# A graph network on one Trainium2 core: an attention table built head by head in other PSUM banks, and routing with bf16 counts and one-hots shared by two engines

## What is computed

```python
# layer 0 attention, 4 heads
f1 = einsum('hno,ho->hn', support, weight_u)      # support = inputs @ weight, by heads
f2 = einsum('hno,ho->hn', support, weight_v)
w = leaky_relu(f1[:, None, :] + f2[:, :, None], 0.2)
e = where(adj != 0, exp(w * adj - row_max), 0)
out = (e / sum(e)) @ support + ...
# layer 0 experts: 16, the best 2 for each row
gate_logits = x @ gate_w + gate_b
topk_vals, topk_idx = top_k(gate_logits, 2)
topk_w = softmax(topk_vals)
y = x + sum_k topk_w * (relu(x @ w1[e_k] + b1[e_k]) @ w2[e_k] + b2[e_k])   # then a layer norm
```

## Time and profile before

| | us |
|---|---|
| median of 3 runs | 2665.99 |
| lowest, highest | 2665.8, 2669.86 |
| the profiled execution | 2668.27 |
| its span, first to last instruction | 2666.3 |
| mean granted TensorE clock in the span | 0.964 |

### The profile page before, as it was taken

One profiled execution on the slowest core, in us unless ns is written; L12 is line 12 of the kernel. 1 busy time (PEld: TensorE's weight loads), 2 busy tenths in 40 slices (PEclk: granted clock), 3 DMA queues, 4 the chain that ended last, 5 costly groups with the idle time before them and its releaser, 6 DMA issues. The chain is left out here.

```text
span 2666.3 us, 57932 instructions
## 1 busy us (share of the span) xinstructions
PE 2475.0 (93%) x20164; PEld 2013.1 (76%) x20165; DVE 1996.3 (75%) x4252; ACT 1622.0 (61%) x3061; POOL 1422.0 (53%) x1705
## 2 busy tenths in 40 slices
PE   7799999999976997189999999999799999999999
PEld 6477777777755997176777777777588888888887
DVE  6799999999935443888877777777677777777775
ACT  1677777777731332246666666666577777777775
POOL 8566666666342553522222221112278888888886
PEclk9899999999987999599999999999799999999999
DMA  3011111111063223301111111110000000000001
GB/s 101 22 43 64 43 43 43 64 44 43 22 227 138 71 70 93 103 7 43 43 42 42 42 45 59 42 42 21 7 0 0 0 0 0 0 0 0 0 0 42
DMA packets 43751, 114.01 MB, mean 43 GB/s; under 512 B 5509, under 2 KB 29806, under 8 KB 37870
## 3 DMA queue, kind: packets, MB, share of 16 engines
q1 hardware_dynamic: 38062, 97.16, 10.4%
q0 software_dynamic: 5568, 15.21, 1.9%
HBM read 99.20 MB, written 13.15 MB: 42 GB/s over the span
## 5 line engine op out<-in xcount | busy, mean ns | idle before, releaser
L2270 PE MATMUL f_pm<-f_wl,f_yt 128*128 128x256 f32 x2640 | 625.4, 380 | 1.9 <-DVE f_gg L2099 1.9
L2270 PEld LDWEIGHTS f_pm<-f_wl,f_yt 128*128 128x128 f32 x2640 | 477.0, 191 | 54.0 <-issue 2.4
L1144 POOL TENSOR_TENSOR ADJ<-ADJ,OFF 128x2708 f32<-128x2708 f32 x21 | 125.3, 5965 | 539.7 <-DVE ADJ L1224 539.7
L120 POOL TENSOR_SCALAR f_yy<-f_th,f_rs 128x255 f32<-128x255 f32 x660 | 370.7, 577 | 21.8 <-POOL f_rs L115 21.8
L2099 DVE SCALAR_TENSOR_TENSOR f_gg<-f_th,f_pm 128x512 f32<-128x512 f32 x319 | 218.9, 686 | 173.8 <-ACT f_th L2213 172.6
L561 ACT COPY a_wt<-a_tp 128x512 f32<-128x512 f32 x528 | 256.6, 566 | 147.3 <-PE a_tp L777 147.2
L670 DVE SCALAR_TENSOR_TENSOR a_lg<-a_f1s,F2S,a_fo 128x1024 f32<-128x1024 f32 (+1 forms) x264 | 296.5, 1152 | 32.0 <-PE a_fo L764 30.8
L589 POOL TENSOR_SCALAR OFF<-ADJ 128x677 bf16<-128x677 f32 x84 | 284.4, 3410 | 63.1 <-DMA ADJ<-in_adj 63.1
L1204 DVE CUSTOM_DVE_ANT_0 a_sc<-a_qk,ADJ 128x1024 f32<-128x1024 f32 (+1 forms) x264 | 288.1, 1093 | 34.2 <-PE a_qk L1314 33.9
L2213 ACT ACTIVATE f_th<-f_pm 128x512 f32<-128x512 f32 x319 | 190.6, 597 | 195.8 <-PE f_pm L2270 195.8
L1168 ACT ACTIVATE a_sc<-a_sc,a_mx 128x1024 f32<-128x1024 f32 (+1 forms) x264 | 277.7, 1052 | 34.7 <-DVE a_mx L1209 34.7
(11 more groups left out here) (323 smaller groups left out, 4518.7 us busy)
## 6 DMA issues: line engine op xcount, KB each, us to landing
ADJ<-in_adj SPq DMA_DIRECT2D x44, 1354.0 KB, 5.9
W<-in_L_ffn_w SPq DMA_DIRECT2D x32, 512.0 KB, 9.8
m_got<-YD SPq DMA_DIRECT2D x6, 768.0 KB, 10.6
out<-X SPq DMA_DIRECT2D x21, 128.0 KB
XD<-XF SPq DMA_DIRECT2D x3, 768.0 KB
m_b<-in_L_ffn_b SPq DMA_DIRECT2D x1, 2048.0 KB, 9.6
X<-in_x SPq DMA_DIRECT2D x1, 1024.0 KB, 10.4
m_rows<-XD,SLOT POOLq DMA_INDIRECT x58, 2.8
```

The costliest lines, as they stand in the source:

```text
L120: return eng.tensor_scalar(out, x, rs[:, 0, bass.ds(t, 1)], rs[:, 1, bass.ds(t, 1)], ALU.mult, ALU.add)
L2270: mm = pe.matmul(out, yt[:, g, r, k, :], wl[:, k, :], start=(k == 0), stop=(k == KD - 1))
```

## The change

It joins four edits.

1. The table `f1s` is made in pieces of at most 512 columns, six for each head, through the three banks `tp` that the transposes use later. TensorE's order mixes them with the logits of units 0 and 1. VectorE makes the first three pieces of head 0, ScalarE all others: up to head 2 ahead of its first exp, head 3 behind it. `leaky` waits for the pieces that it reads.
2. In routing, `ones`, `before`, `pick`, `cnt`, `cm`, `rise` and `past` are bf16 instead of f32; `cm` moves into the buffer `xt`.
3. `in_row` of quarters 2 and 3 is made by ScalarE: (row - place)^2 by 11 Square activations, then relu(1 - that), which is 1 where they are equal and 0 elsewhere. `in_row` has three buffers.
4. The product with `lo`, which differs only for the last tile's column, is by a per-partition scalar (two instructions in quarters 1 and 3), and goes ahead of the product with `hi`.

```diff
@@ layer0_attention @@
+        pieces = [(c0 + n0, min(512, cn - n0)) for c0, cn in CHUNKS for n0 in range(0, cn, 512)]
+        per_chunk = len(pieces) // NC
+
+        def table_ready(eng, end):
+            for b in range(TB):
+                if some((end + TB - 1 - b) // TB):
+                    eng.wait_ge(f1s_done[b], (end + TB - 1 - b) // TB)
...
@@ ScalarE @@
-                for n in range(first, end, 2):
-                    act.wait_ge(spread[0], n // 2 + 1)
-                    c0, cn = CHUNKS[n % NC]
-                    act.activation(f1s[:, n // NC, c0:c0 + cn], fo[:, 0, 0:cn], ACT.Identity,
-                                   scale=SLOPE).then_inc(f1s_done[0], 1)
-            table(0, 2 * NC)
+                for n in range(first, end):
+                    act.wait_ge(spread[n % TB], n // TB + 1)
+                    c0, cn = pieces[n % len(pieces)]
+                    act.activation(f1s[:, n // len(pieces), c0:c0 + cn], tp[:, n % TB, 0:cn], ACT.Identity,
+                                   scale=SLOPE).then_inc(f1s_done[n % TB], 1)
+            table(len(pieces) // 2, 3 * len(pieces))
             exp_part(Unit(0, 0, 0, 0))
-            table(2 * NC, H * NC)
+            table(3 * len(pieces), H * len(pieces))
...
@@ VectorE, in leaky @@
+                if not unit.later(-H) and h == 0:
+                    table_ready(dve, (c + 1) * per_chunk)
+                elif not unit.later(-H) and c == 0:
+                    table_ready(dve, (h + 1) * len(pieces))
...
-            table(1, 2 * NC)
+            table(0, len(pieces) // 2)
             for h in range(2):
                 for c in range(NC):
                     leaky(Unit(0, 0, h, h), c)
-                if h == 1:
-                    table(2 * NC + 1, H * NC)
                 mask(Unit(0, 0, h, h))
...
@@ TensorE @@
+                    if n >= TB:
+                        pe.wait_ge(f1s_done[n % TB], n // TB)
+                    c0, cn = pieces[n % len(pieces)]
+                    pe.matmul(tp[:, n % TB, 0:cn], SEL[:, n // len(pieces), :], FP[:, c0:c0 + cn],
+                              start=True, stop=True).then_inc(spread[n % TB], 1)
+            for c in range(NC):
+                table(c * per_chunk, (c + 1) * per_chunk)
+                logits(Unit(0, 0, 0, 0), c)
+            table(len(pieces), 2 * len(pieces))
+            for c in range(NC):
+                logits(Unit(0, 0, 1, 1), c)
+                if c == 1:
+                    table(2 * len(pieces), 3 * len(pieces))
+            table(3 * len(pieces), H * len(pieces))
             for c in range(2):
                 logits(Unit(0, 0, 2, 2), c)
+            table_ready(pe, H * len(pieces))
             over_units(pe, step)
...
@@ moe_route, ScalarE @@
+            act.wait_ge(place_ok, 1)
+            for q in range(2, 4):
+                if q == 3:
+                    act.wait_ge(act_row_ok, 1)
+                    act.wait_ge(slot_mm, 1)
+                for j in range(NQ):
+                    act.activation(away[:, j, :], rows_i[:, :], ACT.Square, scale=-1.0,
+                                   bias=posf[:, 1, q * NQ + j:q * NQ + j + 1]).then_inc(away_ok, 1)
+                act.wait_ge(away_ok, (q - 1) * NQ)
+                act.activation(in_row[:, q % 3, :, :], away[:, :, :], ACT.Relu, scale=-1.0,
+                               bias=1.0).then_inc(act_row_ok, 1)
...
@@ moe_route, VectorE, in a quarter @@
-                for r, part in enumerate((hi, lo)):
-                    dve.tensor_tensor(named[:, q % 2, :, r, :], in_tile[:, q % 2, :, :],
-                                      part[:, q // 2, q % 2 * NQ:(q % 2 + 1) * NQ].rearrange(
-                                          "p (j a) -> p j a", a=1).to_broadcast([P, NQ, XTILES]),
-                                      ALU.mult).then_inc(named_ok, 1)
+                k, first = divmod(q * NQ, NT)
+                whole = NQ - (1 if first + NQ == NT else 0)
+                dve.tensor_scalar(named[:, q % 2, 0:whole, 1, :], in_tile[:, q % 2, 0:whole, :], lo[:, k, 0:1], None,
+                                  ALU.mult)
+                if whole < NQ:
+                    dve.tensor_scalar(named[:, q % 2, whole, 1, :], in_tile[:, q % 2, whole, :],
+                                      lo[:, k, NT - 1:NT], None, ALU.mult)
+                dve.tensor_tensor(named[:, q % 2, :, 0, :], in_tile[:, q % 2, :, :],
...
```

More of the change, by code:

```diff
@@ L725, in table @@
             def table(first, end):
-                for n in range(first, end, 2):
-                    dve.wait_ge(spread[1], n // 2 + 1)
-                    c0, cn = CHUNKS[n % NC]
-                    dve.tensor_scalar(f1s[:, n // NC, c0:c0 + cn], fo[:, 1, 0:cn], SLOPE, None,
-                                      ALU.mult).then_inc(f1s_done[1], 1)
-                for s in range(2):
-                    dve.wait_ge(f1s_done[s], end // 2)
-            table(1, 2 * NC)
+                for n in range(first, end):
+                    dve.wait_ge(spread[n % TB], n // TB + 1)
+                    c0, cn = pieces[n]
+                    dve.tensor_scalar(f1s[:, 0, c0:c0 + cn], tp[:, n % TB, 0:cn], SLOPE, None,
+                                      ALU.mult).then_inc(f1s_done[n % TB], 1)
+            table(0, len(pieces) // 2)
             for h in range(2):
```

65 lines of the change are left out of this document (28 added, 37 removed).

## The result

| | before | after |
|---|---|---|
| median of 4 runs, us | 2666.01 | 2650.98 |
| lowest, highest | 2665.8, 2669.86 | 2650.11, 2654.48 |
| the profiled execution | 2668.27 | 2650.11 |
| its span | 2666.3 | 2648.2 |

After over before is 0.9938, with a 95% interval of 0.9926 to 0.995: 15.0 us or 0.6% faster in the medians, and the interval leaves out 1. The prediction was 2651.2 in a range of 2647.5 to 2657.7.

The account below looks back on a forecast made before the run. Bound where touched: engines waiting on each other at attention's start, with VectorE pacing, and VectorE at routing's end. 6.5 + 8.3 = 14.8 us off 2668.27 gives 2653.5; the median lies 2.3 lower: 2651.2, range 2647.5 to 2657.7.

Parts of the forecast that it names:

- Rival 4: Attention: the start's gain is lost before TensorE's bound, say on GpSimd's tables; only 8.3 us remains, 2657.7; chance 0.05.
- The attention's term: Attention's start: table by heads brings unit 2's third leaky chunk from 101.72 to 95.2; gain 6.5 us, range 3.7 to 8.6.
- middle case: Attention's start: TensorE's clock high, falling during the exp, back after some 5 us of dense work; gain 6.5 us.
- Rival 1: Attention's start: clock stays low throughout; attention gains 3.7 us, in all 12.0, 2654.0; chance 0.10.
- all high: Attention's start: TensorE's clock high throughout, unit 2's third leaky chunk at 93.1; gain 8.6 us.
- Rival 3: Attention's table: ScalarE's pieces take 0.65 us each instead of 0.49; total gain 12.2 us, 2653.8; chance 0.08.
- The counts: Routing: bf16 counts and products bring VectorE's base from 799.35 to 794.55; gain 4.8 us, 4.2 to 5.2.
- The one-hots: Routing's end: VectorE loses two in_row and gets cheaper lo products, 15.3 to 11.0 us; gain 4.3, from 2.6 to 4.5.
- ScalarE's half: Routing's one-hots: 11 squares (3.3 us) and a Relu (1.4) per quarter, ending 1.3 us before VectorE's last product.
- Rival 2: Routing's one-hots: ScalarE is late, squares 0.59 us each; gain 4.0 us there, in all 10.5, 2655.5; chance 0.08.
- The cap by the XD copies: Routing's end: SyncE's XD copies, DMA ending at 812.9, cap the 9.1 us gain at 8.4 or 8.5; 8.3 taken.
- Rival 5: Attention's first units: TensorE stays at low clock, up to 7.4 us more per unit; three give 2673.5, slower; chance 0.03.

Follow-up runs that it names:

- table alone: Kernel before with only the new attention table, routing as before: median 2658.03 us, ratio 0.9961 to before.
- XD ahead: Kernel after with SyncE's stores to XD issued behind half of the expert weights' loads instead of all: median 2647.74 us, ratio 0.9921.
- filler: Kernel after with three needless VectorE multiplications ahead of its last routing steps: median 2655.13 us, inconclusive as a total; routing stage 59.49 us.
- kept at work: Kernel after with 12 needless TensorE matmuls during ScalarE's exp of unit 0: 2652.67 us in one run.
- blockwise: Kernel after with table pieces of heads 0 and 1 in one block, heads 2 and 3 in another, as in before's order: 2652.85 us in one run.
- counts alone: Kernel before with only routing's bf16 types and cm in the other buffer, one-hots as before: 2663.51 us in one run.
- routing alone: Kernel before with the change's routing, attention table as before: median 2660.84 us, ratio 0.9972 to before.
- both edits: Kernel after with XD's stores earlier in SyncE's queue and unit 0's exp behind the whole table: median 2647.29 us, ratio 0.9926.
- `lo` edit: XD ahead with the lo products put back from the scalar to the broadcast form: 2648.18 us in one run.

## Why the prediction was right, point by point

**What bounds the kernel, and that a shift goes through: right.** The reading that VectorE's unit 2 sets everything behind it is the table above: the rest is 654.36 or 654.37 in all seven kernels with the new table. Rival 4 (the gain lost on GpSimd's tables) would show there and does not.

**The attention's term: right in its chain, too small.** 6.5 with a range of 3.7 to 8.6. Against single executions the gain is 8.75, outside that range. With all of them, third chunks of 32.56 on the mean of three with the old table and 23.12 on the mean of four with the new order (after, table alone, XD ahead, filler) make 9.44, less 0.15: 9.3. The step that was mis-sized, by the times of after set 0.19 later to match the prediction's clock:
- The exp was to end at 87.4 and its banks to be used from 89.1 on; unit 2's logits started at 87.5, 1.6 us earlier. Some 0.75 of it is the clock at the start. I let the high level come back at about 77; the granted clock was 0.86 in 73 to 74 and 1.00 from there. In the table-alone kernel it came back at 76, about as I had assumed, and the last three pieces start 17.16 us after the stage's start instead of 16.41. The other 0.85 I put down to many small estimates (six pieces 2.94 where they take 2.74, each handover a little high); it was not taken apart.
- Two chunks of logits at the low level: 3.5 predicted, 3.24 measured. Transposes and third chunk: 2.6 predicted, 2.07 measured, since the clock was back at 0.91 in 90 to 92. 0.8 us.

1.6 and 0.8 are the 2.4 by which 95.2 stood too late against 92.8. The middle case itself, high, then a fall in the exp, then a return, was what happened. Rival 1 (low all through) did not: but the rise is not at a fixed place, see below. The "all high" bound of 8.6 (third chunk 23.1 after the start) is passed by after itself, with 22.79 in spite of its fall, and by the 21.33 of the kernel kept at work, so it was no bound: the small estimates stood in it too.

**ScalarE's pieces: right.** Six pieces in 2.74, of which one has 148 columns, is 0.49 for each of 512; 12 pieces in the blockwise kernel take 5.51. Rival 3 (0.65 each) falls. A single piece is 0.60 long in the trace, but the next starts 0.49 behind it. The estimate of 0.57 from the Trainium skill (VectorE: DVE Perf Modes, section on the TRN2 errata) is near the length of one piece; as a distance it is too long, and the measurement decides.

**The counts: right.** 4.8 predicted, 4.93 measured (8.73 less 3.80), 3.81 again with the counts alone.

**The one-hots: right, with one step mis-sized.** 4.3 predicted, 4.0 measured (15.35 less 11.37). The `lo` product of 11 by 58 is 0.45 apart and not 0.3; the one of 10 by 58 is 0.28, plus 0.15 for the extra column. I had taken 0.3 each, plus 0.1 for a column. That makes 1.76 for the four instead of 1.4, and is the difference. The Trainium skill (VectorE: DVE Perf Modes, "What auto-detection actually checks") has a rule on outermost dimensions that are even or equal, which I could not weigh from the trace of before. Here 638 elements take 0.45 and 580 take 0.28; by the elements alone 638 would take 0.31. So the shape with 11 is the slower one for each element, though source and target both have 11 there, which the rule as stated would let pass; the trace does not decide how the rule applies. It does show that this shape is far from the 0.73 of the broadcast form.

**ScalarE's half: right.** 11 squares in 3.32 and a Relu of 1.38; predicted 3.3 and 1.4. The cover, between the second Relu's end and VectorE's last product, is 1.6 where 1.3 was predicted. Rival 2 falls.

**The cap by the XD copies: right as a mechanism, mis-sized.** The chain gave 8.9 (4.93 and 4.0; predicted 9.1). The cap was set at 8.4 or 8.5 "from DMA's end at 812.9 and a barrier of about 1". The failed step is the first of the two. The barrier was right: it takes 1.1 from the end of SyncE's wait (804.9 to 806.04), and 1.16 from the start of VectorE's last instruction. But 812.9 is where the DMA share fades, to 0.09 and not to nothing, and SyncE's wait ends 1.0 later, at 813.9. With 813.9 and a barrier of 1.0 to 1.16 the next stage could not begin before 814.9 to 815.1, and the cap comes out at 7.3 to 7.5, from the trace of before alone. Measured: with the mean of before's and the table-alone kernel's routing, 66.1, and the 59.0 of after and routing alone, the term is 7.1 and not 8.3 (7.38 between the two first executions). The XD-ahead kernel shows the other side: 57.08, a term of 9.0, which is the uncapped chain. The Trainium skill (DMA: Bandwidth & Descriptors, "Anatomy of one DMA — SWDGE (gpsimd) path") says that most of a transfer's fixed cost of about 2 us is the receipt that the last byte has landed, before its semaphore can fire. It says so of GpSimd's transfers, and these are SyncE's: from the last traffic (804.6) to the end of SyncE's wait (804.9) the trace has 0.3 us, so no run here shows a receipt of that length.

**The sum.** 6.5 and 8.3 make 14.8; the measured terms are 9.3 and 7.1, together 16.4, and the medians say 15.0 with an interval of 13.3 to 19.7. The errors, plus 2.8 and minus 1.2, partly cancel, and scatter does the rest: against the medians of before in the two larger sets of runs, 2668.22 and 2667.58, the kernel after is 17.2 and 16.6 faster. The nearness of 2651.2 to 2650.98 is luck. Rival 5 (slower, by a low level in the units proper) is excluded by the constant rest.

**What stays open.** The experts' stage was 230.76 to 231.26 in the three kernels with XD ahead (alone, with both edits, with the `lo` edit) and 232.22 to 235.57 in all others. In the three, VectorE's first long wait there, for a bias that DMA brings, is 6.8 to 7.2 us against 8.3 to 9.4, and the bias lands 7.9 us after its issue against 9.0 to 10.2. So XD ahead seems to give 1 to 2 us more in the next stage, by a load that lands sooner; why it does was not tried.

## What to carry to other kernels

Find the first instruction behind which the engine that sets the pace no longer waits, and time a start by that row alone: here one leaky chunk 23 us after the start fixed the length of a stage of 677 to 0.03 us, and made every edit readable in one execution, where totals scattered by some 4 us. When a stage ends for two engines, read each one's end from its own wait: the fade of the DMA share stood 1 us ahead of the end of SyncE's wait, and the barrier behind either engine took the same 1.1 or 1.2. The cheapest fix was to issue the copies earlier in their queue. What an edit gains beyond such a cap is lost until the cap goes: on top of the counts, the one-hots brought 2.6 us (61.61 to 59.06) with XD behind, and 4.5 (61.61 to 57.08) with XD ahead. Some 0.6 of both lies ahead of the picks, where nothing was edited: their end comes 34.1 to 34.8 us after the stage's start in different executions.
